# A fused decoder layer on one core: gate logits read off the cross products instead of the normed rows

## What is computed

```python
x = layernorm(x + self_attention(x))                   # 16 heads of 16, one shared K and V head
x = layernorm(x + softmax(q' k'^T / 16 + mask) @ ctx)  # q', k' = the same two linear maps; 120 context rows
gate_logits = x @ Wg.T                                 # 8 experts
top 2 of softmax(gate_logits), renormed -> comb
x = layernorm(x + sum_e comb_e * (((x W1_e)a * sigmoid((x W1_e)b)) @ Wo + bo))
```

## Time and profile before

| what | value |
|---|---|
| time, median of 3 runs | 1426.19 us (1421.70 to 1429.67) |
| the profiled execution's own time | 1429.21 us |
| its span, first to last instruction | 1427.4 us |
| mean granted TensorE clock | 0.971 |
| PE, DVE, ACT, POOL busy | 1276.7, 1147.2, 743.8, 641.3 us |
| DMA moved | 237.57 MB, mean 166 GB/s |

### The profile page before, as it was taken

How to read it: one execution, slowest core, us unless ns; L and a number is a source line. 1 busy time by engine, 2 the same in 40 slices (tenths; PEclk the granted TensorE clock), 3 DMA queues, 4 the chain that set the end, 5 groups by cost and what they waited for, 6 DMA issues and landing times.

```text
span 1427.4 us, 30146 instructions
## 1 busy us (share of the span) xinstructions
PE 1276.7 (89%) x7734; PEld 900.9 (63%) x7735; DVE 1147.2 (80%) x3145; ACT 743.8 (52%) x1740; POOL 641.3 (45%) x978
## 2 busy tenths in 40 slices
PE   6888899999989999999988659999999999968886
PEld 4443556555555565555554448888888888858786
DVE  0457688988889889889887658888888888859998
ACT  1226677777777777777776312222222222214444
POOL 3002244554445545554544433333333333348886
PEclk9999999999999999999999769999999999989999
DMA  7646476775765756757655764433344433379995
GB/s 176 139 97 112 121 152 147 165 174 139 161 143 142 160 140 151 147 143 161 132 132 193 291 225 135 134 128 131 132 134 134 134 129 130 132 268 335 329 340 190
DMA packets 182817, 237.57 MB, mean 166 GB/s; under 512 B 21376, under 2 KB 144256, under 8 KB 176960
## 3 DMA queue, kind: packets, MB, share of 16 engines
q1 hardware_dynamic: 158864, 169.50, 47.2%
q0 software_dynamic: 17488, 55.02, 10.2%
q10 hardware_dynamic: 6368, 11.89, 2.4%
HBM read 138.34 MB, written 98.30 MB: 166 GB/s over the span
## 4 chain that ended last, share of the span: by engine, by line
PE 61%; DVE 16%; issue 8%; DMA 6%; ACT 4%; POOL 2%; SPq 2%; DVEq 0%; ACTq 0%; POOLq 0%
PE psO L617 6%; PE psHb L1390 5%; PE psHb L1387 5%; PE psHb L1386 5%; PE psS L724 5%; PE psHa L1386 4%; PE psHa L1387 4%; PE psHa L1390 4%; PE psB L646 4%; PE psT L734 4%; DVE negmax L1022 3%; DVE x2in L1582 3%; DMA qstack<-q_parts 3%; PE psO L568 2%; PE psX L1410 2%
## 5 line engine op out<-in xcount | busy, mean ns | idle before, releaser
L1022 DVE TENSOR_REDUCE negmax<-psS 128x2 f32<-128x512 f32 x512 | 349.7, 687 | 83.6 <-PE psS L724 66.1
L863 ACT ACTIVATE probs<-psT 128x512 f32<-128x512 f32 x512 | 303.2, 598 | 159.7 <-PE psT L734 144.1
L1467 ACT ACTIVATE sig<-hb 128x512 f32<-128x512 f32 x135 | 85.4, 632 | 287.0 <-DVE hb L1540 283.3
L724 PE MATMUL psS<-kstack,qstack 96*128 96x256 bf16 x1024 | 195.4, 273 | 37.6 <-DVE kstack L1120 13.4
L734 PE MATMUL psT<-qstack,kstack 99*128 99x512 bf16 x512 | 194.1, 381 | 4.6 <-ACT probs L863 4.5
L1349 POOL DMA_INDIRECT g_rows<-g,slot x135 | 134.4, 995 | 70.0 <-issue 66.7
L724 PEld LDWEIGHTS psS<-kstack,qstack 96*128 96x128 bf16 x1024 | 92.5, 104 | 94.0 <-DVE negmax L1022 36.5
L477 POOL DMA_INDIRECT lists<-x,slots x128 | 128.3, 1003 | 33.9 <-issue 30.1
L617 PE MATMUL psO<-probs,vaug 128*32 128x512 f32 x1024 | 138.4, 613 | 0.4 <-ACT probs L863 0.4
L1551 DVE SCALAR_TENSOR_TENSOR g<-g,xe,sig 128x512 f32<-128x512 f32 x135 | 101.5, 752 | 26.1 <-DVE g L1547 16.4
L1540 DVE TENSOR_TENSOR hb<-psHb,b 128x512 f32<-128x512 f32 x135 | 93.4, 692 | 32.2 <-issue 28.8
(11 more groups left out here) (207 smaller groups left out, 2953.2 us busy)
## 6 DMA issues: line engine op xcount, KB each, us to landing
rows<-g_rows SPq DMA_DIRECT2D x32, 1024.0 KB, 8.0
qstack<-q_parts SPq DMA_DIRECT2D x192, 128.0 KB
xe<-lists SPq DMA_DIRECT2D x135, 133.0 KB, 2.1
q_parts<-qpart SPq DMA_DIRECT2D x32, 384.0 KB
sums<-x SPq DMA_DIRECT2D x32, 264.0 KB
x2in<-sums SPq DMA_DIRECT2D x32, 264.0 KB, 4.9
xt<-in_x_t SPq DMA_DIRECT2D x32, 256.0 KB
part_raw<-in_f_t SPq DMA_DIRECT2D x32, 256.0 KB, 5.1
```

Source lines behind the costliest of these rows:

```text
L724: last = mm(psS[:, u % 2, hh * S:(hh + 1) * S], qstack[0:KROWS, b1.s4, 2 * hp + hh, c * P:(c + 1) * P], kstack[0:KROWS, b1.s4, :], start=T ...
L863: nc.scalar.activation(probs[:, u % PT, :], psT[:, u % 2, :], ACT.Exp, scale=SELF_SCALE).then_inc(sm["exp_done"], 1)
L1022: v.tensor_reduce(negmax[:, b1.s2, 2 * hp:2 * hp + 2, c], psS[:, u % 2, :].rearrange("p (h k) -> p h k", h=2), AX.X, ALU.max, negate=True) ...
```

## The change

- `keymap` gets 8 more columns for each batch: the gate matrix with its column means taken off. The cross product then also gives x1 @ Wg', which DVE copies into 8 extra columns of x1 (slot 4).
- A new small load brings the transposed context of the batch (`ctxt`, rows of 480 bytes); PE multiplies it by the centred gate matrix in slot 9, ACT copies the result into 8 extra columns of ctxv, and the cross attention's value product, now 264 columns, one half in `psA` and one in `psB`, yields y2 with 8 extra columns: the logits before the scaling by rstd.
- The transposes of x2, their copy, the product with Wg and the copy of the logits are gone. Top eight and indices are taken of the unscaled columns (slots 6 and 7); the exponentials scale by rstd (ACT, slots 8 and 9), with a maximum that POOL scales by one more instruction after rstd and shift.
- The statistics of the two halves of y2 are taken in slots 0 and 1 and aggregated in slot 2; x2 is normed in slots 5 and 6. Counts go to `psO[:, 0]`, when draining to `psB`.
- POOL waits for the slots only at its dispatch. When draining, counts, slots, the store of x2 and the dispatch come within the step itself; there is one step less (38).

```diff
-        for n in range(B + 7):
+        for n in range(B + 6):
...
+            if active(t.back(6)) and draining(t):
+                store_x2(t.back(6))
...
+        def scale_max(b):
+            wait(pool, "rstd2_ready", 4 * b.n + 2)
+            pool.tensor_tensor(gneg[:, b.s2], uneg[:, b.s2], rstd2[:, b.s2], ALU.mult).then_inc(sm["rstd2_ready"], 1)
...
             elif active(b6):
-                rstd(b6, "var2_ready", mv2, vare2, nmean2, rstd2, shift2, "rstd2_ready")
+                wait(pool, "gate_exp", done(b6.back(2)))
+                rstd(b6, "var2_ready", mv2, vare2, nmean2, rstd2, shift2, "rstd2_ready", per=4)
+                scale_max(b6)
...
-                wait(pool, "slots_ready", done(b7))
...
+            if active(b6) and draining(t):
+                dispatch(b6, 0)
+                dispatch(b6, 1)
...
+            for k in range(DC):
+                mm(psT[:, 0, DC:DC + E], ones[:, :], wg[:, k, :], start=k == 0, stop=k == DC - 1)
...
-                            last = mm(psA[:, c * SC:(c + 1) * SC], x1t[:, b5.s2, k, c * P:(c + 1) * P],
-                                      keymap[:, k, bass.ds(b5.n * SC, SC)], start=k == 0, stop=k == DC - 1)
+                            last = mm(psA[:, c * (SC + E):(c + 1) * (SC + E)], x1t[:, b5.s2, k, c * P:(c + 1) * P],
+                                      keymap[:, k, b5.n, :], start=k == 0, stop=k == DC - 1)
...
-                if u == 5 and active(b6):
-                    wait(pe, "x2_ready", done(b6))
-                    bank_read(bank_b, t, "x2_transposed")
...
-                if u == 7 and active(b6):
-                    wait(pe, "x2t_copied", done(b6))
-                    bank_read(bank_b, t, "gate_scored")
...
+                    wait(pe, f"ctxt_loaded{b5.s2}", 16 * b5.half + 16)
+                    for k in range(DC):
+                        last = mm(psB[0:SC, S:S + E], ctxt[:, b5.s2, k, :], wgc[:, k, :],
+                                  start=k == 0, stop=k == DC - 1)
...
+                    bank_read(bank_b, t, "cross_out")
                     for c in range(QC):
-                        last = mm(psA[:, c * D:(c + 1) * D], cprob_t[:, b5.s2, c * P:(c + 1) * P], ctxv[:, b5.s2, :],
+                        last = mm((psA, psB)[c][:, 0:D + E], cprob_t[:, b5.s2, c * P:(c + 1) * P], ctxv[:, b5.s2, :],
...
+            v.scalar_tensor_tensor(wgc[:, :, :], psT[:, 0, DC:DC + E].unsqueeze(1).to_broadcast([P, DC, E]), -1.0 / D,
+                                   wg[:, :, :], ALU.mult, ALU.add)
+            for k in range(DC):
+                v.scalar_tensor_tensor(keymap[:, k, :, SC:SC + E],
...
+                if u == 1 and active(b6) and not draining(t):
+                    v.bn_stats(stats2[:, b6.s2, 1, :], y2[:, b6.s2, 1, 0:D]).then_inc(sm["stats2_ready"], 1)
                 if u == 1 and active(b6):
+                    wait(dve, "gate_exp", done(b6.back(2)))
+                    v.tensor_reduce(uneg[:, b6.s2], y2[:, b6.s2, :, D:D + E], AX.X, ALU.max, negate=True)
+                if u == (1 if draining(t) else 2) and active(b6):
                     moments(stats2, mv2, b6, "var2_ready")
...
+                    v.tensor_copy(x1[:, b5.s2, :, D:D + E], both[:, :, SC:SC + E]).then_inc(sm["raw_copied"], 1)
```

More of the change, by code:

```diff
@@ L367, in step @@
                 load_setup()
[L368 to L373, removed]
+            if active(t.back(7)) and t.n <= B + 1:
+                store_x2(t.back(7))
             b = t.back(3)
@@ L500, in step @@
                 expert_constants()
-            if active(b7):
-                if not active(t):
-                    wait(pool, "slots_ready", done(b7))
+            late = active(b7) and t.n <= B + 1
+            if late:
                 dispatch(b7, 0)
@@ L779, in copy_keymap, with norm @@
                 load_context_group(act, g + 2)
-        def norm(x, rs, shift, y, b, ready, name):
-            wait(act, ready, done(b, 3))
-            for c in range(QC):
-                last = nc.scalar.activation(x[:, b.s2, c, 0:D], y[:, b.s2, c, :], ACT.Identity,
+        def norm(x, rs, shift, y, b, ready, name, per=3, half=None):
+            wait(act, ready, per * b.n + 3)
+            for c in range(QC) if half is None else (half,):
+                last = nc.scalar.activation(x[:, b.s2, c, 0:D], y[:, b.s2, c, 0:D], ACT.Identity,
                                             scale=rs[:, b.s2, c:c + 1], bias=shift[:, b.s2, c:c + 1])
-            last.then_inc(sm[name], 1)
+            if half != 0:
+                last.then_inc(sm[name], 1)
         def copy_att(b, g):
@@ L837, in step @@
                     wait(act, "cross_out", done(b5.back(2)))
+                    copy(ctxv[:, b5.s2, D:D + E], psB[0:SC, S:S + E])
                     copy(cprob_t[:, b5.s2], psB[0:SC, 0:S]).then_inc(sm["cprobt_copied"], 1)
-                if u == 11 and active(b6):
-                    wait(act, "gate_max", done(b6))
-                    wait(act, "comb_ready", done(b6.back(2)))
-                    for c in range(QC):
-                        nc.scalar.activation(gexp[:, b6.s2, c, :], logits[:, b6.s2, c, :], ACT.Exp,
-                                             bias=gneg[:, b6.s2, c:c + 1], accum_out=gsum[:, b6.s2, c:c + 1])
-                        last = nc.scalar.activation(gtop[:, b6.s2, c, :], top[:, b6.s2, c, 0:2], ACT.Exp,
-                                                    bias=gneg[:, b6.s2, c:c + 1])
-                    last.then_inc(sm["gate_exp"], 1)
                 if u == 12 and active(t):
@@ L1144, in step @@
             if active(b6):
-                gate(7)
-                wait(dve, "hot_ready", done(b6))
-                for c in range(QC):
-                    v.scalar_tensor_tensor(x2[:, b6.s2, c, D:D + E], gexp[:, b6.s2, c, :],
-                                                  gden[:, b6.s2, c:c + 1], hotsum[:, b6.s2, c, :], ALU.mult, ALU.mult)
-                v.tensor_copy(x2[:, b6.s2, :, D + E + 1], topf[:, b6.s2, :, 0]).then_inc(sm["comb_ready"], 1)
-                if not b6.fixed or b6.n >= 2:
-                    v.tensor_scalar(x2[:, b6.s2, :, D + E], x2[:, b6.s2, :, D + E], float(4 * S), None, ALU.add)
-                wait(dve, "counted", done(b6))
-                wait(dve, "slot_link", 3 * b6.n - 2)
-                count = psB[:, 0:3 * E].rearrange("p (c e) -> p c e", e=E)
-                now, then = base[:, b6.s2, :], base[:, 1 - b6.s2, :]
-                v.tensor_tensor(place[:, b6.s2], count[:, 0:QC, :], now.unsqueeze(1).to_broadcast([P, QC, E]), ALU.add)
-                v.tensor_tensor(then, count[:, QC, :], now, ALU.add).then_inc(sm["slot_link"], 1)
+                gate_slot(t, b6, UNITS)
         pipeline(dve, step)
```

286 lines of the change are left out of this document (166 added, 120 removed).

## The result

| what | before | after |
|---|---|---|
| time, median of 20 runs each, on one chip | 1428.0 us (1421.46 to 1436.34) | 1434.49 us (1428.0 to 1441.14) |
| ratio after to before | | 1.0044, 95% interval 1.0026 to 1.0062 |
| span of the profiled execution | 1427.4 us | 1433.3 us |
| slot 0 of steps 8 and 32 on PE | 211.41, 739.16 us | 211.25, 738.71 us |
| last batch's slots written (DVE) | 831.77 us | 838.52 us |

The forecast was 1412.0, the range 1401 to 1428: the change is slightly slower, where 14 us less were forecast. The last three lines say where: the steady part gave nothing (527.75 us between steps 8 and 32 before, 527.46 after), and the end of the pipeline lost 7.2 us (from 739.16 to 831.77 before, 92.61; from 738.71 to 838.52 after, 99.81).

What follows compares the result with a forecast made beforehand. Waits between PE and DVE were taken to close most steps (21.82 us), the q loop five; 14.5 us gained in steady steps, 1.8 lost at the start, 1.5 gained draining: 14.2 off, 1412.0 us against 1426.19, range 1401 to 1428.

Steps and rivals of the forecast that it cites:

- The terms on PE: Steady step up to slot 11: wait 0.87, transposes 0.49, gate product 0.81 saved, less 0.40 and 0.05: 1.72 us earlier.
- the start: Before the steady steps: two more small products, 0.8 us, and three DVE instructions ahead of cvec, about 1.0: 1.8 us lost.
- base step: Steady step's usual length, forecast to fall from 21.82 to 21.0 us, 18.0 us over 22 steps.
- the hand-over: Slots 5 to 8: DVE leads by its maxima's banks and hands PE only 0.8 of its 1.72 us by slot 11.
- I take nothing, with 0.3 a step as the other end: Cost of moving the gate's exponentials on ACT from slot 11 to 8 and 9, as ACT is least loaded.
- The wait of DVE for POOL: Draining steps: rstd behind four scatters comes some 3.6 us later and blocks DVE's norm in slot 3.
- 2 to 4 us each: Draining steps t = 34 to 37: PE's gain per step from removed work, against up to 3.6 us lost.
- POOL later by 0.3: Steady step behind slot 0: POOL's split of q starts 0.3 us later, all of it going into q's loop.
- The q loop: From PE's slot 0 through SP's store of q and reads back to landing: 20.3 to 20.9 us, setting five steps.
- 2 of the 18: Steady part: 2 us of the 18 gained taken back for steps where a held DMA shows, bounds 0 and 10.
- rival A: q's loop takes 21.5 us in most steps, freed time becomes a qstack wait at slot 0: 1422 us; 0.23 with E.
- Rival E: PE's removed wait is replaced by another at the same slot, psS's bank not being free; 0.23 together with A.

Runs made afterwards that it cites:

- e1: Changed kernel with the gate exponentials back in slot 11 and DVE's three steps to the weights' reciprocal one slot later; 1425.85 us, ratio to before 1.0007.
- e2: Changed kernel with the last part of the maxima's split behind the cross scores in steady steps; 1432.22 us, ratio to before 1.006.
- e3: Changed kernel with both edits: gate exponentials back in slot 11, last part of the maxima's split behind the cross scores; 1433.87 us, ratio to before 1.0058.
- e4: Changed kernel with draining steps' scatters behind the next step's rstd, as before the change, except in the last step; 1426.16 us, ratio to before 1.0016.
- e10: e3 with the transposed context loaded for the first two batches alone, so later batches read old data; 1432.07 us, ratio to before 1.0043.
- e7: e3 run once more, as its added PE products stood under a condition never met; 1431.96 us, ratio to before 1.0045.
- e6: e3 plus scatters in the old order, key columns' copies behind the first spread, and POOL's q split ahead of rstd; 1420.65 us, ratio to before 0.9956.

## Why the prediction was wrong

**The terms on PE were right.** The transposes with their wait gave 1.46 us in slot 5 (0.87 + 0.49 = 1.36 taken), the gate product 0.81 between slots 6 and 7 (0.81 taken); the context's product costs 0.34 us in the step shown (575.54 to 575.88), 0.40 taken. PE's lead in slot 7 is nevertheless 1.42 us and not 2.2, as a new wait of 0.81 stands ahead of slot 6.

**Where the 20 us between forecast and result lie.** On the profiles a gain of 14.2 was forecast and a loss of 5.9 measured. The steady part was to gain 14.5 and gained 0.3; the draining part was to gain 1.5 and lost 6.4 (7.2, less 0.8 behind it); the start was to lose 1.8 and, up to step 8, gained 0.2. The base step was to be 21.0 and is 21.84: 0.39 of that is ACT's, 0.45 the hand-over's.

**The first step that failed is "I take nothing, with 0.3 a step as the other end", on ACT.** It rested on ACT's mean load of 37.91 in 50. But slots 7 to 11 are its full stretch, `cprob_t` stands at its end, and the k projection waits for that copy's bank. Four activations with their two reads of sums, moved there, put the copy late. e1 prices it: 0.39 us a step, 8.6 us in 22 steps. The prediction even said that the slots were the fullest, and then went by the mean.

**The hand-over of 0.8 was too large, and at another bank: the second step that failed.** It was right that DVE leads from slot 5 to 8, by the split's last part that ends with POOL's instruction. But the price was taken from the maxima's banks. The stricter wait, which the prediction doesn't name, is the one in `psA`, where slot 6's product needs the cross scores read; it sums to 17.9 us in the 500 us, where the removed wait had 19.2. With the exponentials out of the way (e1) PE keeps 0.51 us at slot 11, and the step gains 0.37, not 0.82. e2 and e3 confirm the place: with the cross scores first another 0.44, and with both edits the base step is the 21.0 that was forecast.

The Trainium skill, SBUF — State Buffer, "Who interferes with whom", gives the exclusion of DVE and GpSimd that this rests on. The traces agree further: L970 takes 0.79 us in the mean with POOL later, and ends with POOL's instruction at 572.28 and 572.23; the other runs bear it out (last section).

**Draining was outside its bounds: the third step that failed.** The wait of DVE for POOL was forecast at 3.6 us a step, and 3.5 to 4.3 was found. What was mis-sized is what the steps gain in return: 2 to 4 us each were taken. The kernel after lost 7.2 us where 1.5 gained and at worst 5 lost stood. With the scatters out of the way (e4) the draining part took 86.3 us against 92.6 before, a gain of 6.3 over all of it: about 1 to 1.5 a step, not 2 to 4. The place of the scatters took 13.5.

**What held.** POOL later by 0.3 and the store with it (9.57 against 9.25); the start, as far as can be told, with the first maximum 1.9 us later (45.20 against 43.30; 1.8 forecast), though that is partly luck: the same place is at 44.47 to 47.04 in the runs that share this start, and step 8 begins no later than before; the stretch from slot 11 to slot 0; the new load's DMA at nothing (e10). The q loop at 20.3 to 20.9 us in most steps was about right. But the slack was not enough for its late cases: once the base step was 21.0 (e3), the "2 of the 18" for held DMAs became 1.1 us a step, some 24 us (bounds 0 and 10). So the steady part would not have gained its 14.5 us even with the first two steps right: e3 has the forecast's base step, and its mean step is 22.08 us against 21.97 before.

**By the rivals.** The steady steps stayed at 21.8, as rival A's test had it ("the maxima come at 21.8 a step"), but not by its cause: from step 8 on no step waits longer for `qstack` than before (1.52 against 1.80 us at most). The 0.44% lie within the half per cent that was called no change, with a chance of 0.21, though the interval leaves out 1. Rival E's kind of thing happened, a bank in place of the removed wait, yet in `psA` and `psB`, not `psS`. The sum of the measured terms on the profiles: steady -0.3, start and first steps -0.2, draining +7.2, behind it -0.8: +5.9, the difference of the spans. Each is from one execution of each kernel, and the start alone scatters by 2 us between e3 and e7.

## What to carry to other kernels

When an operation is moved on an engine that is lightly loaded on average, read that engine's timeline between the two neighbours of the new place and name who waits for the next copy there; a mean load says nothing of it. When a wait is removed, list for every bank and buffer behind it who must have read it and when, and take the latest of them; here 0.81 us a step came back one slot behind the 0.87 removed. And before shortening a step, measure the loop that runs beside it with its scatter, not its usual value: in e2 and e3 a step shorter than the loop's late cases gave back all that it had gained.

## What the runs showed of the hardware

PE's granted clock can fall behind a single short wait: in e3 it is 1.00 up to a wait of 2.38 us for a DMA and 0.64 in the 3.7 us behind it, with products between at 1.2 GHz. Of e3's seven waits of 1.66 to 2.86 us for `qstack` with transposes behind them, five were followed by four transposes in 1.09 to 1.12 us and two (1.75 and 2.14 us) by four in 0.66. In e7 a wait of 1.40 us had a fall behind it, in e10 two of 2.29 and 2.70 us had none. So the length of the wait alone does not tell it.

The gate's exponential of 8 columns takes 0.39 us in the change, where it has a scale for each row beside the bias, and took 0.29 without one (and with its input in another buffer), as ACT's timeline of the kernel before has it:

```profile
424.64 0.29 ACT L843 ACTIVATE gexp<-logits,gneg 128x8 f32<-128x8 f32 x1
...
424.92 0.28 ACT L845 ACTIVATE gtop<-top,gneg 128x2 f32<-128x2 f32 x1
```

With four of them that is 0.4 us of ACT a step, none of it in the forecast.

The 0.79 us of L970, for 32 numbers in a row, are DVE standing still until POOL's instruction is through. The instruction takes as long as is left of POOL's: 0.65 us before, 0.79 after, 0.39 in e3 and 0.26 in e6, where it starts later, and in each of these kernels it ends 0.04 to 0.06 us behind POOL's in all the 24 or 25 steps between 200 and 738 us.
